# Causal mask of two attention stages: added by VectorE with the row maximum, in place of mask products on TensorE

## The chip, the cores and the metric

The kernel runs on one core of a Trainium2 chip. Five engines work side by side, each through its own queue in order: TensorE (PE in the profile; its weight loads are listed as PEld), VectorE (DVE), ScalarE (ACT), GpSimd (POOL), and SyncE (SP), which here only issues DMAs. They wait for each other by semaphores. The metric is the time of one execution on the device in microseconds (us); the kernel before has a median of 3226.27 us.

## The reference

Two transformer layers follow each other on x of 16 sequences x 512 tokens x 128 channels: a gated state-space block, a latent attention (16 heads of 8), a routed SwiGLU expert layer, a plain causal attention (16 heads of 8), a routed GELU expert layer, each with a residual and a layer norm. The two attentions are what the change touches:

```python
# latent attention (layer 0), kk and qq are [no-rope 4 | rope 4] per head
scores = jnp.einsum('bqhd,bkhd->bhqk', qq, kk) * scale
causal = jnp.tril(jnp.ones((S, S), dtype=bool))
scores = jnp.where(causal[None, None], scores, jnp.finfo(scores.dtype).min)
probs = jax.nn.softmax(scores, axis=-1)
y = jnp.einsum('bhqk,bkhd->bqhd', probs, v).reshape(B, S, H)
...
# plain attention (layer 1)
scores = jnp.einsum('bhqd,bhkd->bhqk', q, k)
causal = jnp.tril(jnp.ones((S, S), dtype=bool))
scores = jnp.where(causal[None, None], scores, jnp.asarray(MASK_BIAS, scores.dtype))
attn = jax.nn.softmax(scores.astype(jnp.float32), axis=-1).astype(dt)
ctx = jnp.einsum('bhqk,bhkd->bqhd', attn, v)
```

## The kernel before

The stages run one after the other. Both attentions are the function attention_stage: tiles named mla_... belong to the latent one, mha_... to the plain one. A sequence of 512 tokens is four blocks of 128 rows. The 16 heads are four groups g of four heads (NG = HG = 4), and one turn (one sequence) is the four groups in order; 16 turns make a stage, so a stage has 64 groups, two stages 128.

The softmax is done in two passes over the scores, one group apart and two groups apart:

- First pass, for group g: the products Q K^T with the queries as rows, cut to the causal width: row block j has w = 128 (j + 1) keys. They are 16 products (scores, L1394), packed into 11 units (UNITS1): unit 0 has four heads of 128 keys, units 1 and 2 two heads of 256, units 3 to 6 one head of 384, units 7 to 10 one head of 512. A unit fills one PSUM bank; three banks rotate (S1), so TensorE can be three units ahead of VectorE (semaphores s1_ready and s1_free). The last matmul of each unit (L1398) adds the causal mask: identity times a 128 x 128 triangle of 0 and -1e30, on the last 128 keys of every head of the unit. VectorE then takes the negated row maximum of every head in the bank by one TENSOR_REDUCE per unit (L1101) into nm.
- The maxima of the group are split by GpSimd into two parts (nhl), transposed by TensorE (L1441) to rows, copied by VectorE (mhl, L1068) and carried by a DMA into two further rows of Qb.
- Second pass, two groups later: K Q^T with the keys as rows and these two rows included, so that the score less its maximum comes out (scores_less_max, L1406), 16 products in 10 units (UNITS2), in two PSUM banks (s2_free, s2_ready). ScalarE takes the exponential (L1297), and GpSimd zeroes what lies above the diagonal (mask_unit, L1216); it is told by e_seen that an exponential is finished. Then come the products with V (times_v, L1414), a selection product that turns them back (L1446), and VectorE's division (normalise, L1073 and L1074).

The order on each engine is written out by hand. TensorE goes through k = 0 to 10 in each group and issues scores(k) and then scores_less_max(k). At k = 4 (WIDE) come the transposed maxima, the selection product and the first half of the products with V; at k = 8 the second half. The work that prepares the next sequence lies in between: in group 0 at k = 6 the latent projection (latent stage only), in group 1 at k = 0 and k = 6 the key and query projections and at k = 4 the output product, in group 2 at k = 7 the value projection, in group 3 at k = 4 a transpose of x. VectorE goes through the same k: the maximum of unit k, at k = 4 L1068, L1073 and L1074, and in between the rotation (turn_rows: L1052, L1053, L1055), the low parts (L1046, L1059, L1040), the output sum (L1086) and the statistics (L105, L108, L1035, L1036).

## Time and profile before

| | |
|---|---|
| median of 3 runs | 3226.27 us |
| lowest, highest | 3219.61, 3237.03 us |
| the profiled execution | 3232.98 us, its span 3231.2 us |
| TensorE, busy share of the span | 81% |
| VectorE | 67% |
| ScalarE | 44% |
| GpSimd | 36% |
| mean granted TensorE clock | 0.919 |

The span is the time from the first to the last instruction. "Busy" is the time in which at least one instruction's record is open on an engine; records of neighbouring instructions overlap, so the distance from one start to the next is shorter than a record. The latent attention lies between about 550 and 1385 us of the span, the plain one between about 1900 and 2690 us.

### The profile page before, as it was taken

How to read it: one execution, taken by the hardware profiler on the slowest of the kernel's cores; microseconds unless marked ns; L12 is line 12 of the kernel's file. 1: busy time of each engine (PE TensorE's matmuls, PEld its weight loads, DVE VectorE, ACT ScalarE, POOL GpSimd, SP SyncE). 2: the span in 40 equal slices, each digit the busy share in tenths (PEclk: the TensorE clock that was granted, in tenths of full speed). 3: DMA queues.
4: the chain of work that ended last, by engine and by line, in shares of the span. 5: the costliest groups of instructions: out<-in, count | busy, mean ns of one | idle time of the engine just before them, and what ended most of it. 6: DMA issues, size and time to landing. Idle time of an engine off the chain costs nothing. (4 is left out here: it accounts for less than half of the span.)

```text
span 3231.2 us, 51537 instructions
## 1 busy us (share of the span) xinstructions
PE 2618.4 (81%) x17479; PEld 2011.4 (62%) x17479; DVE 2178.6 (67%) x5628; ACT 1414.6 (44%) x2412; POOL 1177.9 (36%) x2298
## 2 busy tenths in 40 slices
PE   1445873999999999948888759999999997698972
PEld 1423662777777777636666647777777766486861
DVE  5733773777777767448888846676767754677785
ACT  0001330455555555511111225666666652586861
POOL 3210110334434344322222113454455442773076
PEclk9997995899999999969999969999999995799996
DMA  2144001213223222031110032222122114697772
GB/s 29 32 134 127 23 13 30 41 29 44 42 29 47 37 34 41 15 104 50 49 49 32 3 43 33 31 40 36 25 40 40 26 17 165 231 296 225 250 218 73
DMA packets 198657, 228.02 MB, mean 71 GB/s; under 512 B 48621, under 2 KB 148814, under 8 KB 190478
## 3 DMA queue, kind: packets, MB, share of 16 engines
q1 hardware_dynamic: 188302, 207.69, 26.7%
q0 software_dynamic: 8192, 16.79, 1.6%
q10 hardware_dynamic: 2048, 2.10, 0.2%
q8 instruction: 60, 0.98, 0.1%
q14 instruction: 55, 0.45, 0.0%
HBM read 132.55 MB, written 58.10 MB: 59 GB/s over the span
## 5 line engine op out<-in xcount | busy, mean ns | idle before, releaser
L1394 PE MATMUL banks<-Kb,Qb 96*128 96x128 f32 (+3 forms) x2048 | 599.6, 348 | 58.6 <-issue 27.3
L1406 PE MATMUL banks<-Qb,Kb 98*128 98x512 f32 (+3 forms) x2048 | 602.7, 356 | 4.8 <-ACT mha_prob L1297 1.0
L1101 DVE TENSOR_REDUCE mha_nm<-banks 128x1 f32<-128x384 f32 (+3 forms) x704 | 421.5, 639 | 185.9 <-PE banks L1398 172.3
L1101 DVE TENSOR_REDUCE mla_nm<-banks 128x1 f32<-128x384 f32 (+3 forms) x704 | 419.9, 638 | 160.0 <-PE banks L1398 146.5
L1297 ACT ACTIVATE mla_prob<-banks 128x512 f32<-128x512 f32 x640 | 376.5, 598 | 311.6 <-PE banks L1406 303.2
L1394 PEld LDWEIGHTS banks<-Kb,Qb 96*128 96x128 f32 x2048 | 364.3, 195 | 216.5 <-issue 159.9
L1297 ACT ACTIVATE mha_prob<-banks 128x512 f32<-128x512 f32 x640 | 375.7, 598 | 273.7 <-PE banks L1406 260.8
L1216 POOL TENSOR_SCALAR_AFFINE_SELECT mla_prob<-mla_prob 128x256 f32<-128x256 f32 (+1 forms) x640 | 237.8, 379 | 405.3 <-PE banks L1394 379.7
L1406 PEld LDWEIGHTS banks<-Qb,Kb 98*128 98x128 f32 x2048 | 334.8, 193 | 47.1 <-issue 7.6
L1216 POOL TENSOR_SCALAR_AFFINE_SELECT mha_prob<-mha_prob 128x256 f32<-128x256 f32 (+1 forms) x640 | 225.6, 361 | 355.4 <-PE banks L1394 329.2
L1828 PE MATMUL banks<-glu_wd,glu_hid 128*128 128x128 f32 x1024 | 147.7, 288 | 74.3 <-DVE glu_hid L1707 74.1
L1828 PEld LDWEIGHTS banks<-glu_wd,glu_hid 128*128 128x128 f32 x1024 | 130.5, 196 | 117.6 <-DVE glu_hid L1707 113.8
L2174 DVE TENSOR_TENSOR moe_hl<-moe_h,moe_hh 128x512 fp32r<-128x512 f32 x212 | 146.4, 692 | 78.7 <-ACT moe_h L2278 65.7
L1788 ACT ACTIVATE glu_sg<-banks 128x512 f32<-128x512 f32 x128 | 76.4, 597 | 262.2 <-PE banks L1802 262.2
L2277 ACT ACTIVATE moe_hh<-banks,moe_bt 128x512 fp32r<-128x512 f32 x212 | 146.1, 689 | 87.7 <-PE banks L2291 72.3
L1398 PE MATMUL banks<-mla_mask,mla_identr 128*128 128x128 f32 (+2 forms) x704 | 183.8, 261 | 0.0
L2227 POOL DMA_INDIRECT moe_gb<-results,moe_back_slot x128 | 131.2, 1025 | 143.5 <-SPq L1988 105.6
L1398 PE MATMUL banks<-mha_mask,mha_identr 128*128 128x128 f32 (+2 forms) x704 | 181.5, 258 | 0.0
L1414 PE MATMUL banks<-mla_prob,mla_V 128*9 128x512 f32 (+3 forms) x2048 | 169.1, 450 | 0.3
L1414 PE MATMUL banks<-mha_prob,mha_V 128*9 128x512 f32 (+3 forms) x2048 | 167.4, 446 | 0.2
L2214 POOL DMA_INDIRECT slots<-X,moe_slot x128 | 126.5, 988 | 67.3 <-issue 38.7
L1398 PEld LDWEIGHTS banks<-mla_mask,mla_identr 128*128 128x128 f32 x704 | 139.2, 198 | 8.5
(434 smaller groups left out, 5392.1 us busy)
## 6 DMA issues: line engine op xcount, KB each, us to landing
moe_wt<-expert_rows SPq DMA_DIRECT2D x53, 1024.0 KB
conv_tz<-conv_kernel SPq DMA_DIRECT2D x16, 1024.0 KB, 6.8
moe_xg<-slots SPq DMA_DIRECT2D x53, 256.0 KB
results<-moe_yt SPq DMA_DIRECT2D x53, 256.0 KB
Kb<-mla_kh SPq DMA_DIRECT2D x32, 256.0 KB, 4.9
Qb<-mla_qh SPq DMA_DIRECT2D x128, 64.0 KB
Kb<-mha_kh SPq DMA_DIRECT2D x32, 256.0 KB, 5.6
Qb<-mha_qh SPq DMA_DIRECT2D x128, 64.0 KB
```

The lines of the kernel that those rows point to most:

```text
L1101: dve.tensor_reduce(nm[:, g % 2, h:h + heads, j], ps[:, bank1(g, k), 0:heads * w].rearrange("p (h k) -> p h k", h=heads), axis=AX.X, op=AL ...
L1216: pool.affine_select(out=part, in_=part, compare_op=ALU.is_ge, fill=0.0, base=0, pattern=pattern, channel_multiplier=-1).then_inc(p_ready, 1)
L1297: act.activation(prob[:, g % 2, k, :], ps[:, S2 + k % 2, :], ACT.Exp, scale=HD ** -0.5).then_inc(s2_free, 1)
L1394: one = pe.matmul(ps[:, bank, x * w:(x + 1) * w], Qb[0:MROW, u, g, h + x, j * P:(j + 1) * P], Kb[0:MROW, u, g, 0:w], start=(x == 0), stop= ...
L1398: pe.matmul(ps[:, bank, 0:heads * w].rearrange("p (x w) -> p x w", x=heads)[:, :, w - P:w], identr[:, :], mask[:, 0:heads, :], start=False ...
L1406: last = pe.matmul(ps[:, S2 + k % 2, at:at + w], Kb[0:MROW + 2, u, grp, kb * P:(kb + 1) * P], Qb[0:MROW + 2, u, grp, h, kb * P:L], start=T ...
L1414: last = pe.matmul(ps[32 * hh:32 * hh + HD + 1, OB, kb * P:L], V[:, u, kb, grp * HG + hh, :], prob[:, par, unit, at:at + w], start=(kb == ...
L1828: last = pe.matmul(ps[:, OB + e % 2, b * P:(b + 1) * P], hid[:, e % 2, b * P:(b + 1) * P], wd[:, e, :], start=True, stop=True)
L2174: dve.tensor_tensor(hl[:, k, :], h[:, k, :], f32(hh[:, k, :]), ALU.subtract).then_inc(hid_ready, 1)
L2214: pool.indirect_dma_start(slots_d, bass.IndirectOffsetOnAxis(slot[:, q, a, t:t + 1], 0), X[:, first + j, b, :], None).then_inc(scattered[q ...
L2227: pool.indirect_dma_start(gb[:, j % 2, a, b, :], None, res_d[q], bass.IndirectOffsetOnAxis(back_slot[:, q, a, t:t + 1], 0)).then_inc(gathe ...
L2277: act.activation(hh[:, k, :], ps[:, FB + k, :], ACT.Gelu_apprx_tanh, bias=bias)
```

## The change

In scores the mask product and its constant tiles go: the identity identr and the four-fold mask. The products of a unit are now each a closed group of their own (start and stop both true), and the last one tells s1_ready. The mask becomes one tile of 128 x 512: zeros, and the triangle in the last 128 columns, so that its last w columns are the mask of any row block.

On VectorE the one TENSOR_REDUCE of a unit is replaced by one tensor_tensor_reduce for each head: it adds the last w columns of the mask to the head's scores from PSUM, multiplies by -1, and takes the minimum of that along the row, which is the negated maximum. The sum itself is written to a tile that nobody reads (junk, bfloat16). A unit's bank is freed with its last head. Such an instruction is compiled to two: the pass over the row, and one that writes the result to nm.

The signal e_seen, which rode on the first score product of the next unit, is now an instruction of its own on TensorE's queue, behind the wait for s2_free.

```diff
-        mask, identr = N.sb("mask", [P, HG, P], F32R), N.sb("identr", [P, P], F32R)
+        mask, junk = N.sb("mask", [P, L]), N.sb("junk", [P, 3, L], BF16)
...
-                sp.dma_start(maskf, io["c_mask"]).then_inc(consts, 16)
+                sp.dma_start(mask[:, L - P:L], io["c_mask"]).then_inc(consts, 16)
...
+                link(dve.memset(mask[:, 0:L - P], 0.0))
...
-                link(dve.tensor_copy(mask[:, :, :], maskf.unsqueeze(1).broadcast_to([P, HG, P])))
-                link(dve.tensor_copy(identr[:, :], ident[:, :]))
...
-                                w = P * (j + 1)
-                                dve.tensor_reduce(nm[:, g % 2, h:h + heads, j],
-                                                  ps[:, bank1(g, k), 0:heads * w].rearrange("p (h k) -> p h k", h=heads),
-                                                  axis=AX.X, op=ALU.max, negate=True).then_inc(s1_free, 1)
+                                w, bank = P * (j + 1), bank1(g, k)
+                                for x in range(heads):
+                                    last = dve.tensor_tensor_reduce(
+                                        junk[:, S1.index(bank), x * w:(x + 1) * w], ps[:, bank, x * w:(x + 1) * w],
+                                        mask[:, L - w:L], -1.0, BIG, ALU.add, ALU.min, nm[:, g % 2, h + x, j:j + 1])
+                                last.then_inc(s1_free, 1)
...
                     for x in range(heads):
                         one = pe.matmul(ps[:, bank, x * w:(x + 1) * w], Qb[0:MROW, u, g, h + x, j * P:(j + 1) * P],
-                                        Kb[0:MROW, u, g, 0:w], start=(x == 0), stop=False, skip_group_check=True)
-                        if seen and x == 0:
-                            one.then_inc(e_seen, 1)
-                    pe.matmul(ps[:, bank, 0:heads * w].rearrange("p (x w) -> p x w", x=heads)[:, :, w - P:w],
-                              identr[:, :], mask[:, 0:heads, :], start=False, stop=True,
-                              skip_group_check=True).then_inc(s1_ready, 1)
+                                        Kb[0:MROW, u, g, 0:w], start=True, stop=True)
+                    one.then_inc(s1_ready, 1)
...
                     pe.wait_ge(s2_free, c.next(s2_free))
+                    pe.sem_inc(e_seen, 1)
```

TensorE, latent stage, the last unit of group 0 and the first two of group 1 in one turn of the loop. Before:

```order
L1394 MATMUL banks<-Kb,Qb 128x512 [waits mla_s1_free]
L1398 MATMUL banks<-mla_mask,mla_identr 128x128
L1394 MATMUL banks<-Kb,Qb 128x128 [waits mla_s1_free,mla_m_rows1]
L1394 MATMUL banks<-Kb,Qb 128x128 x3
L1398 MATMUL banks<-mla_mask,mla_identr 128x512
L1406 MATMUL banks<-Qb,Kb 128x512 [waits mla_s2_free]
```

The same place of the changed kernel:

```order
L1396 MATMUL banks<-Kb,Qb 128x512 [waits mla_s1_free]
L1396 MATMUL banks<-Kb,Qb 128x128 [waits mla_s1_free,mla_m_rows1]
L1396 MATMUL banks<-Kb,Qb 128x128 x3
L1405 MATMUL banks<-Qb,Kb 128x512 [waits mla_s2_free]
```

The mask products between the first-pass products and the second-pass ones are gone; nothing else moved.

VectorE, latent stage, units 0 to 4 of group 1. Before:

```order
L1101 TENSOR_REDUCE mla_nm<-banks 128x4 [waits mla_s1_ready]
L1101 TENSOR_REDUCE mla_nm<-banks 128x2 [waits mla_s1_ready] x2
L1052 TENSOR_TENSOR mla_xs<-banks,mla_sinr 128x512 [waits mla_k_ready]
L1053 TENSOR_TENSOR mla_tmp<-banks,mla_cosr 128x512
L1055 TENSOR_TENSOR mla_tmp<-mla_tmp,mla_xs 128x512 [waits mla_done]
L1101 TENSOR_REDUCE mla_nm<-banks 128x1 [waits mla_s1_ready] x2
```

The changed kernel, from the second head of unit 2 on (the first head of a unit is the row with the wait; ISA is the name of the new instruction's two parts):

```order
L1102 ISA mla_junk,mla_nm<-banks,mla_mask 128x256 [waits mla_s1_ready]
L1102 ISA mla_nm 128x1
L1102 ISA mla_junk,mla_nm<-banks,mla_mask 128x256
L1102 ISA mla_nm 128x1
L1052 TENSOR_TENSOR mla_xs<-banks,mla_sinr 128x512 [waits mla_k_ready]
L1053 TENSOR_TENSOR mla_tmp<-banks,mla_cosr 128x512
L1055 TENSOR_TENSOR mla_tmp<-mla_tmp,mla_xs 128x512 [waits mla_done]
L1102 ISA mla_junk,mla_nm<-banks,mla_mask 128x384 [waits mla_s1_ready]
L1102 ISA mla_nm 128x1
L1102 ISA mla_junk,mla_nm<-banks,mla_mask 128x384 [waits mla_s1_ready]
L1102 ISA mla_nm 128x1
```

Where one row stood for a unit, two now stand for each of its heads: 32 instructions in a group for 11, at the same places between the other work.

## Rows read from the trace of the kernel before

**Rows 1.** The page: busy time of each engine, and its second part, 40 slices.
```profile
PE 2618.4 (81%) x17479; PEld 2011.4 (62%) x17479; DVE 2178.6 (67%) x5628; ACT 1414.6 (44%) x2412; POOL 1177.9 (36%) x2298
PE   1445873999999999948888759999999997698972
```

**Rows 2.** Windows, latent stage: groups 0 to 3 of one turn (columns: stretch, length, busy).
```profile
core 0: us, PE busy (x) PEld busy (x) DVE busy (x) ACT busy (x) POOL busy (x), PEclk, DMA share, GB/s
800.17:813.00 12.83, 12.83 (x98) 9.73 (x97) 8.63 (x17) 8.26 (x15) 3.75 (x12) 1.00 0.00 1
813.00:827.73 14.73, 13.92 (x105) 10.43 (x104) 12.34 (x23) 7.51 (x14) 5.01 (x14) 1.00 0.16 39
827.73:838.15 10.42, 10.42 (x86) 7.84 (x85) 9.41 (x26) 5.83 (x11) 7.39 (x16) 1.00 0.60 80
838.15:850.66 12.51, 11.72 (x95) 8.85 (x94) 7.97 (x15) 7.70 (x14) 5.45 (x18) 1.00 0.32 38
```

**Rows 3.** Windows, plain stage: groups 0 to 3 of one turn, same columns.
```profile
2131.02:2141.93 10.91, 10.91 (x90) 8.29 (x89) 7.33 (x14) 6.98 (x12) 3.75 (x12) 1.00 0.01 2
2141.93:2155.68 13.75, 13.49 (x105) 10.51 (x103) 10.63 (x26) 9.11 (x16) 4.03 (x13) 1.00 0.06 16
2155.68:2166.97 11.29, 11.29 (x93) 8.66 (x93) 7.30 (x14) 5.97 (x12) 9.96 (x22) 1.00 0.70 91
2166.97:2179.09 12.12, 11.33 (x92) 8.47 (x91) 7.98 (x16) 7.32 (x14) 5.03 (x16) 1.00 0.16 30
```

**Rows 4.** Timeline of TensorE: start, length, line; units with one head, latent stage.
```profile
844.96 0.40 PE L1394 MATMUL banks<-Kb,Qb 96*128 96x512 f32 x1
845.19 0.22 PE L1398 MATMUL banks<-mla_mask,mla_identr 128*128 128x128 f32 x1
845.25 0.48 PE L1406 MATMUL banks<-Qb,Kb 98*128 98x512 f32 x1
845.57 0.39 PE L1394 MATMUL banks<-Kb,Qb 96*128 96x512 f32 x1
```

**Rows 5.** The same view: a bare wait, then units with four and two heads.
```profile
837.04 0.22 PE L1398 MATMUL banks<-mla_mask,mla_identr 128*128 128x128 f32 x1
837.10 0.61 PE L1394 MATMUL banks<-Kb,Qb 96*128 96x128 f32 x4
837.55 0.45 PE L1398 MATMUL banks<-mla_mask,mla_identr 128*128 128x512 f32 x1
837.84 0.40 PE L1406 MATMUL banks<-Qb,Kb 98*128 98x512 f32 x1
...
838.32 0.28 PE L1398 MATMUL banks<-mla_mask,mla_identr 128*128 128x256 f32 x1
838.43 0.45 PE L1406 MATMUL banks<-Qb,Kb 98*128 98x128 f32 x2
```

**Rows 6.** Timeline of VectorE: runs of one instruction close behind each other.
```profile
833.07 0.38 DVE L108 BATCH_NORM_AGGREGATE mla_mv<-mla_st 128x2 f32<-128x6 f32 x4
833.48 0.32 DVE L1035 TENSOR_TENSOR mla_var<-mla_mv 128x4 f32<-128x4 f32 x1
833.84 0.16 DVE L1036 TENSOR_TENSOR mla_var<-mla_var,mla_mv 128x4 f32<-128x4 f32 x1
...
836.72 4.31 DVE L1101 TENSOR_REDUCE mla_nm<-banks 128x1 f32<-128x512 f32 x7 [0.59 <-PE banks L1398]
```

**Rows 7.** Groups of instructions, shapes apart: mean ns behind the comma, latent stage.
```profile
L1101 DVE TENSOR_REDUCE mla_nm<-banks 128x1 f32<-128x512 f32 x224 | 144.3, 684 | 47.4 <-PE banks L1398 44.1
L1101 DVE TENSOR_REDUCE mla_nm<-banks 128x1 f32<-128x384 f32 x223 | 117.3, 553 | 46.3 <-PE banks L1398 46.3
```

**Rows 8.** Timeline of VectorE in group 1, latent stage: where it waits.
```profile
814.59 1.34 DVE L1101 TENSOR_REDUCE mla_nm<-banks 128x2 f32<-128x512 f32 x2 [0.89 <-PE banks L1398]
...
820.74 1.08 DVE L1101 TENSOR_REDUCE mla_nm<-banks 128x1 f32<-128x384 f32 x2 [0.54 <-PE banks L1398]
822.17 0.69 DVE L1059 TENSOR_TENSOR mla_kl<-mla_tmp,mla_kh 128x512 fp32r<-128x512 f32 x1 [0.35 <-ACT mla_kh L1271]
```

**Rows 9.** The page's fifth part: first-pass products, and the time that TensorE waits.
```profile
L1394 PE MATMUL banks<-Kb,Qb 96*128 96x128 f32 (+3 forms) x2048 | 599.6, 348 | 58.6 <-issue 27.3
L1398 PE MATMUL banks<-mla_mask,mla_identr 128*128 128x128 f32 (+2 forms) x704 | 183.8, 261 | 0.0
L1101 DVE TENSOR_REDUCE mla_nm<-banks 128x1 f32<-128x384 f32 (+3 forms) x704 | 419.9, 638 | 160.0 <-PE banks L1398 146.5
```

11 lines of the change are left out of this document (5 added, 6 removed).

## The prediction

> **What bounds the kernel now.** First I read the busy shares and slices [rows 1]: TensorE leads with 81%, and its slices stand at 9 where the two attentions run. That share is no proof, since records of matmuls overlap, so the second view is the windows of one turn of each stage, group by group [rows 2, 3]. They show three kinds of group. In most of them TensorE is busy from edge to edge and VectorE has 3 to 4.5 us of air: latent groups 0 and 3 (12.83 and 12.51 us, VectorE busy 8.63 and 7.97), plain groups 0, 2 and 3 (10.91, 11.29, 12.12 us; 7.33, 7.30, 7.98). TensorE sets their length. In latent group 2 VectorE is busy 9.41 of 10.42 us: both are close. In latent group 1 VectorE is busy 12.34 of 14.73 us, and most of what is left is three waits of 0.89, 0.54 and 0.35 us [rows 8]; here VectorE's extra work (two rotations, low parts, output sum) sets the length. Plain group 1 lies between (10.63 of 13.75). So the change moves work from the engine that bounds five groups in eight to the one that bounds one or two.
>
> **What is removed on TensorE.** The record of a mask product is 0.26 us on average [rows 9], but that is no price: the next matmul starts inside it. From start to start a one-head mask product takes 0.06 us (845.19 to 845.25 [rows 4]), a two-head one 0.11 to 0.12, the four-head one 0.29 (837.55 to 837.84) [rows 5]. Per group: 8 x 0.06 + 2 x 0.12 + 0.29 = 1.0 us. That is the lower bound of the saving where TensorE is the bound. More may go: a second-pass product of 512 columns takes 0.32 us to the next start, a first-pass one of the same width 0.23 [rows 4]; the difference of 0.09 may be a weight load that the short mask product was too short to hide. If all of it went in 10 units the saving would be 1.9 us. I take 1.2, near the lower end, since only the directly read spacing is sure.
>
> **What is added on VectorE.** A run of seven maxima over 512 columns lasts 4.31 us [rows 6], and one record is 0.684 [rows 7], so they follow each other every (4.31 - 0.68) / 6 = 0.605 us. 128 columns more or less are 0.684 - 0.553 = 0.131 us [rows 7], or 1.02 ns a column, so the fixed part is 0.605 - 0.524 = 0.08 us. Columns per group stay the same, 5120. Instructions that pass over a row go from 11 to 16: 5 x 0.08 = 0.40 us. The trace has no instruction that adds and reduces at once; I price its pass like a plain one of the same columns, as both read one PSUM stream, with a second stream from SBUF beside it. New too are 16 writes of the result. The nearest row is a small instruction in a run: four of L108 last 0.38 us with about 0.15 each, so one every 0.08 us [rows 6]. The other bound is a write that overlaps with nothing: the pass is waited for to its record's end (0.684 in place of 0.605) and the write takes a whole small record, 0.16 as L1036 [rows 6], together 0.24. I take 0.08, because no write here has to wait for a semaphore and every run of unlinked instructions in the trace overlaps. 16 x 0.08 = 1.3 us. The addition is 1.7 us per group, 218 us of VectorE in 128 groups, against some 154 us taken off TensorE.
>
> The Trainium skill (VectorE: DVE Perf Modes, "Two Vector instructions with no wait between them") says that an instruction with an accumulator output is two instructions, and that each is held back only where an operand's start quadrant differs from the one used last; all operands here start at partition 0, so by that rule the write overlaps, as I take it. No row of before has such a pair.
>
> One more rule speaks against the change. The seven-fold run gives a fixed part of 0.08 us for a PSUM source [rows 6, 7]. The skill (Perfetto Trace Analysis, "Optimizing Scalar/DVE Operations") puts the overhead of a VectorE instruction at about 125 ns on PSUM. By that the five added passes would cost 0.63 us in place of 0.40; in the three groups where VectorE counts that is 0.7 us a turn, and the forecast would be 3160. The trace disagrees, and I stay with it.
>
> **The signal and the rest.** Ten times per group TensorE's queue now holds a bare wait for s2_free with the signal to GpSimd. A bare wait stands there already ahead of unit 0, and the product behind it starts 0.06 us after the one ahead (837.04 to 837.10 [rows 5]): nothing, as long as the exponential of two units before is done. Units last 0.5 to 0.7 us and an exponential is released two units back, so it is hidden; uncovered it costs at most the 0.05 us or so of a start, 0.5 us per group. GpSimd gets its signal earlier; it has 5 to 9 us of air per group [rows 2]. The constants at the stages' start are under 1 us.
>
> **Group by group.** VectorE's floor is its busy time + 1.7; TensorE's is the length - 1.2 where it sets it. Latent: group 0 12.83 -> 11.6 (VectorE's floor 10.3); group 3 12.51 -> 11.3 (9.7). Group 1: VectorE 12.34 + 1.7 = 14.0, and of its waits the first shrinks, since unit 0 now keeps VectorE 0.6 us longer while TensorE is in the key projection, and the second vanishes as the maxima of units 0 to 4 end later; about 1.0 us remains: 15.0, or +0.3. Group 2: 9.41 + 1.7 = 11.1, with 0.4 of air 11.5, or +1.1. Turn: -1.2 + 0.3 + 1.1 - 1.2 = -1.0 us. Plain: groups 0, 2 and 3 lose 1.2 each (VectorE's floors 9.0, 9.0, 9.7 against 9.7, 10.1, 10.9). Group 1: TensorE's floor 13.49 - 1.2 = 12.3, VectorE's 10.63 + 1.7 = 12.3; two equal loads leave air, I say 13.1, or -0.65. Turn: -4.3 us. With 15 full turns in each stage (the first and last are partial) the sum is 15 x 5.3 = 80 us. The profiled execution took 3232.98 us, so 3153; it was 7 us above the median of 3226.27, so the forecast for a median is 3146 to 3153. I write 3150.
>
> **Rivals.**
> 1. Slower: the write isn't overlapped. At 0.24 us in place of 0.08 for each of 16 pairs VectorE gets 2.5 us more per group, 4.2 in all. Floors: latent 12.8, 16.5, 13.6, 12.2, sum 55.1; with 1 us of air the turn is 5.6 above 50.5. Plain: 11.5, 14.8, 11.5, 12.2, sum 50.0, with 1.5 of air 3.4 above 48.1. 15 x 9 = +135 us: 3360. It turns from gain to loss where a write costs about 0.14 us (5.3 / 14.3 of the way). For it: nothing in the trace has such a pair. Against it: every unlinked run overlaps.
> 2. No change: three banks aren't enough to keep TensorE free. VectorE now needs 0.69 us for a unit of one head and 512 columns, TensorE about 0.5 to 0.55, so TensorE is stopped at every fourth unit, and in turn VectorE stands still during products with V. TensorE waits for VectorE already, a part of the 58.6 us [rows 9]. If two thirds of the gain in the TensorE groups is lost this way (0.4 left of 1.2), the turns change by +0.6 and -1.6 us, 15 us in all; with a few tenths for the bare waits it is zero: 3225.
> 3. Larger: the hidden weight loads go too (1.9 for 1.2). The five TensorE groups give 0.5 more each where VectorE's floor allows it, 15 x 2.3 = 35 us: 3115.
>
> **How the numbers follow.** Forecast 0.54 (own range 3130 to 3195), rival 3 0.08, rival 2 0.18 (3195 to 3245), rival 1 0.20, a third of it between 3240 and 3260 for a write of 0.14 to 0.17 us. The range 3095 to 3260 leaves out most of rival 1 (0.13) and the far end of rival 3 (0.03). Runs tell about 0.5% from no change, 16 us: faster holds the forecast, rival 3 and a quarter of rival 2, 0.67; same 0.12; slower 0.21.
>
> **What the changed profile would show.** VectorE's run of one-head units of 512 columns spaced 0.68 to 0.70 us (rival 1: 0.82 or more); the small write of nm 0.08 us before the next start. TensorE from a first-pass product of 512 columns to the second-pass one 0.23 us. Group lengths as above: latent group 1 and 2 not shorter, plain groups 0 and 2 shorter by a microsecond. The wait of L1396 for VectorE several times what it was; if it eats more than 0.5 us of each TensorE group, rival 2 is it. The prediction is wrong if a pass with two sources costs more per column than 1.02 ns, or if the granted clock, 1.00 in all eight windows [rows 2, 3], drops because TensorE has more air.

## The result, and the profile after

The changed kernel takes 3301.05 us (median of 4 runs, 3282.12 to 3304.74) against 3226.39 us: 1.0217 times as long, with a 95% interval of 1.0168 to 1.0265. A repetition in other runs gave 1.0195 (1.0122 to 1.0269). It is slower; 3150 us and a gain of 2.4% had been forecast. The page of the changed kernel, busy times, slices and three groups:

```profile
PE 2622.3 (79%) x16071; PEld 1894.3 (57%) x16071; DVE 2228.2 (67%) x8314; ACT 1389.0 (42%) x2412; POOL 1157.3 (35%) x2298
...
PEclk9997995898878989969999959899888996799996
...
L1396 PE MATMUL banks<-Kb,Qb 96*128 96x128 f32 (+3 forms) x2048 | 623.6, 364 | 96.9 <-DVE mla_nm L1102 44.2
L1405 PE MATMUL banks<-Qb,Kb 98*128 98x512 f32 (+3 forms) x2048 | 600.9, 357 | 34.4 <-ACT mla_prob L1299 11.5
...
L1102 DVE CUSTOM_DVE_ANT_0 mla_junk<-banks,mla_mask 128x128 bf16<-128x128 f32 (+3 forms) x1024 | 446.2, 487 | 187.3 <-PE banks L1396 156.5
```

TensorE has 1408 matmuls fewer (two stages of 64 groups with 11 mask products), and yet its busy time is 2622.3 us where it was 2618.4 [rows 1]. The products L1396 are 623.6 us in place of 599.6 and their waits 96.9 in place of 58.6 [rows 9]; those of the second pass wait 34.4 us (L1405) in place of 4.8 (L1406 before). Between the eighth and the fifteenth and between the twenty-sixth and the thirty-first slice, where the attentions run, the granted clock reads 8 in nine places and 7 in one; the same line of the kernel before has nines in these places but for the 8 of the eighth:

```profile
PEclk9997995899999999969999969999999995799996
```

The next view says how much that is. Windows over the latent and the plain stage, first of the kernel before, then of the changed one (both from repeated runs on one chip; columns: stretch, length, busy times, clock, DMA):

```profile
553.40:1341.40 788.00, 765.05 (x5722) 576.20 (x5721) 598.83 (x1205) 444.13 (x785) 320.25 (x842) 0.97 0.24 36
1892.70:2639.80 747.10, 733.73 (x5708) 561.94 (x5706) 521.24 (x1057) 450.73 (x785) 340.64 (x898) 0.99 0.22 33
```

```profile
552.10:1386.40 834.30, 767.72 (x5019) 516.32 (x5018) 626.50 (x2549) 433.35 (x785) 308.03 (x842) 0.89 0.23 35
1938.60:2703.40 764.80, 724.30 (x5004) 490.98 (x5003) 544.27 (x2401) 437.43 (x785) 334.24 (x898) 0.92 0.23 33
```

The two stages are 64.0 us longer, about what the whole is (spans of 3222.6 and 3283.8 us; 58.5 us between the medians of all runs of both kernels on that occasion). The mean granted clock fell from 0.97 and 0.99 to 0.89 and 0.92. The clock has two levels, 1.2 and 2.4 GHz, so TensorE ran at the lower one for 41 and 22 us before, and for 180 and 121 us after. One turn of the changed kernel shows where, in windows of its four groups (plain stage, same columns):

```profile
2387.57:2397.93 10.36, 10.27 (x78) 6.78 (x79) 7.11 (x34) 6.27 (x12) 3.84 (x12) 1.00 0.01 2
2397.93:2409.97 12.04, 11.66 (x89) 8.40 (x87) 10.49 (x48) 8.22 (x15) 3.83 (x12) 1.00 0.00 1
2409.97:2424.89 14.92, 14.14 (x85) 9.62 (x86) 7.97 (x37) 6.17 (x12) 10.06 (x22) 0.77 0.58 83
2424.89:2438.68 13.79, 11.91 (x78) 6.92 (x77) 9.39 (x40) 8.16 (x15) 4.67 (x14) 0.88 0.21 27
```

Group 2 of this turn had 6.8 us at half clock and lasts 14.92 us; group 2 at full clock lasts 11.96. So a microsecond at half clock costs 3.0 / 6.8 = 0.44 us. The same sum over all groups with a fall, in all traces of this study, has the median 0.44, with half of the groups between 0.41 and 0.55; for the changed kernel the median is 0.42. I take 0.43. What got longer can be read off the products with V, 3.12 us in place of 1.69, on TensorE, first in group 2 above, then in a group at full clock:

```profile
2416.52 3.12 PE L1413 MATMUL banks<-mha_prob,mha_V 128*9 128x512 f32 x16
...
2217.26 1.69 PE L1413 MATMUL banks<-mha_prob,mha_V 128*9 128x512 f32 x16
```

Now the loss has two parts that must be looked at apart, and every run below is read in the same way. **Turn at full clock**: the length of each kind of group, from TensorE's first product of unit 0 to that of the next group, as the median over those groups in which the clock didn't fall; four of them make a turn. **Half clock**: the time at 1.2 GHz within a stage. For the changed kernel against the one before (12.24, 13.91, 11.76, 11.44 and 10.82, 13.12, 11.91, 11.43 us before):

| group | latent: forecast | measured | plain: forecast | measured |
|---|---|---|---|---|
| 0 | -1.2 | -0.83 | -1.2 | -0.48 |
| 1 | +0.3 | -0.44 | -0.65 | -1.09 |
| 2 | +1.1 | +0.24 | -1.2 | +0.05 |
| 3 | -1.2 | +0.11 | -1.2 | -0.04 |
| turn | -1.0 | -0.92 | -4.3 | -1.56 |

Latent group 2 of the changed kernel was at full clock only three times, so its +0.24 rests on these. At full clock the change gains 2.5 us in two turns, 16 x 2.5 = 40 us, half of the forecast 80. The clock takes (180 + 121 - 41 - 22) x 0.43 = 102 us. The sum is +62, measured +64.

### The profile page after: what moved, and what is told of

It reads as the page before. It is cut to its first block and busy times, and to the rows that moved or that the text cites. A ratio compares the mean times of both kernels' runs of the same rounds, so it can differ in the third digit from the quotient of the medians.

```text
span 3303.0 us, 52641 instructions
## 1 busy us (share of the span) xinstructions
PE 2622.3 (79%) x16071; PEld 1894.3 (57%) x16071; DVE 2228.2 (67%) x8314; ACT 1389.0 (42%) x2412; POOL 1157.3 (35%) x2298
## 5 line engine op out<-in xcount | busy, mean ns | idle before, releaser
L1396 PE MATMUL banks<-Kb,Qb 96*128 96x128 f32 (+3 forms) x2048 | 623.6, 364 | 96.9 <-DVE mla_nm L1102 44.2
L1405 PE MATMUL banks<-Qb,Kb 98*128 98x512 f32 (+3 forms) x2048 | 600.9, 357 | 34.4 <-ACT mla_prob L1299 11.5
L1102 DVE CUSTOM_DVE_ANT_0 mha_junk<-banks,mha_mask 128x128 bf16<-128x128 f32 (+3 forms) x1024 | 443.5, 487 | 196.0 <-PE banks L1396 180.9
L1102 DVE CUSTOM_DVE_ANT_0 mla_junk<-banks,mla_mask 128x128 bf16<-128x128 f32 (+3 forms) x1024 | 446.2, 487 | 187.3 <-PE banks L1396 156.5
L1396 PEld LDWEIGHTS banks<-Kb,Qb 96*128 96x128 f32 x2048 | 378.1, 203 | 294.6 <-issue 170.7
L1405 PEld LDWEIGHTS banks<-Qb,Kb 98*128 98x128 f32 x2048 | 389.1, 205 | 147.3 <-issue 124.6
L1413 PE MATMUL banks<-mla_prob,mla_V 128*9 128x512 f32 (+3 forms) x2048 | 192.7, 500 | 0.0
L1413 PE MATMUL banks<-mha_prob,mha_V 128*9 128x512 f32 (+3 forms) x2048 | 188.0, 490 | 0.0
L2275 ACT ACTIVATE moe_h<-banks,moe_bt 128x512 f32<-128x512 f32 x212 | 144.3, 681 | 0.0
L1685 DVE SCALAR_TENSOR_TENSOR glu_acc<-banks,glu_wts,glu_acc 128x128 f32<-128x128 f32 x448 | 125.4, 342 | 0.2 <-PE banks L1825 0.2
L2286 PE MATMUL banks<-moe_xth,moe_wt 128*128 128x512 f32 x212 | 95.0, 448 | 35.1 <-DVE moe_xtl L2026 35.1
```

The costliest lines, as they stand in the source:

```text
L1102: last = dve.tensor_tensor_reduce(junk[:, S1.index(bank), x * w:(x + 1) * w], ps[:, bank, x * w:(x + 1) * w], mask[:, L - w:L], -1.0, BIG, ...
L1396: one = pe.matmul(ps[:, bank, x * w:(x + 1) * w], Qb[0:MROW, u, g, h + x, j * P:(j + 1) * P], Kb[0:MROW, u, g, 0:w], start=True, stop=True)
L1405: last = pe.matmul(ps[:, S2 + k % 2, at:at + w], Kb[0:MROW + 2, u, grp, kb * P:(kb + 1) * P], Qb[0:MROW + 2, u, grp, h, kb * P:L], start=T ...
L1413: last = pe.matmul(ps[32 * hh:32 * hh + HD + 1, OB, kb * P:L], V[:, u, kb, grp * HG + hh, :], prob[:, par, unit, at:at + w], start=(kb == ...
L2275: act.activation(h[:, k, :], ps[:, FB + k, :], ACT.Gelu_apprx_tanh, bias=bias).then_inc(h_ready, 1)
```

## The experiments

In the first four texts the names of theories are those that each explains; from the fifth on A is ScalarE and the two banks of the second pass, B is VectorE and its three banks, C the clock, and D and S are explained where they stand. All runs, with the ratio to the kernel before on the same occasion. Stages, half clock and turns are read from one traced execution; the last column is from all executions: the half clock of the whole program, 2 x (1 - mean granted clock) x span, its median less that of the kernel before, in us.

| run | ratio, 95% interval | stages, us | half clock, us | turn at full clock, us | half clock, all |
|---|---|---|---|---|---|
| before (b_again) | 1.0019 (1.0000, 1.0038) | 788.0 / 747.1 | 41 / 22 | 49.3 / 47.3 | +7 |
| changed (a_again) | 1.0195 (1.0122, 1.0269) | 834.3 / 764.8 | 180 / 121 | 48.4 / 45.7 | +226 |
| e1_masks_kept | 1.0171 (1.0126, 1.0216) | 835.1 / 769.1 | 87 / 43 | 50.3 / 48.2 | +68 |
| e2_no_mask_products | 0.9997 (0.9972, 1.0023) | 804.1 / 735.4 | 160 / 71 | 47.7 / 45.5 | +172 |
| e3_hybrid | 1.0030 (1.0004, 1.0055) | 819.3 / 736.6 | 160 / 36 | 48.7 / 46.3 | +125 |
| e4_filler | 1.0240 (1.0186, 1.0294) | 872.1 / 760.1 | 237 / 67 | 49.0 / 47.1 | +232 |
| b_exp_half | 0.9932 (0.9910, 0.9954) | 776.4 / 734.8 | 33 / 12 | 48.8 / 46.8 | -16 |
| a_exp_half | 1.0052 (1.0026, 1.0077) | 831.7 / 734.9 | 210 / 100 | - / 44.2 | +231 |
| h1_groups_0_1 | 1.0184 (1.0161, 1.0206) | 854.0 / 745.3 | 194 / 60 | 48.8 / 46.2 | +192 |
| h2_group_1 | 1.0043 (1.0020, 1.0066) | 791.7 / 744.3 | 50 / 38 | 49.4 / 46.8 | +65 |
| h3_masks_0_2 | 1.0224 (1.0194, 1.0255) | 871.8 / 749.3 | 226 / 46 | 49.4 / 47.0 | +199 |
| h4_masks_1_3 | 1.0249 (1.0225, 1.0274) | 859.8 / 762.1 | 205 / 64 | - / 47.1 | +199 |
| i1_new_signal | 1.0005 (0.9992, 1.0018) | 787.6 / 748.9 | 30 / 12 | 49.7 / 47.7 | -10 |
| i2_old_signal | 1.0204 (1.0181, 1.0227) | 832.9 / 760.6 | 190 / 128 | 48.2 / 45.3 | +266 |
| i3_group_1 | 1.0032 (1.0011, 1.0054) | 821.6 / 736.5 | 129 / 34 | 49.3 / 46.4 | +72 |
| j1_plain_1 | 0.9952 (0.9937, 0.9967) | 782.6 / 738.6 | 30 / 40 | 49.4 / 46.4 | -3 |
| j2_plain_1_03 | 0.9946 (0.9929, 0.9962) | 782.7 / 726.3 | 30 / 34 | 49.4 / 45.8 | +13 |

A dash: latent group 2 was at full clock only in the last turn, where part of its work is missing. On the occasions of the e, h and j runs the kernel before takes 3370 us in place of 3226. The excess lies behind the attentions: in j1 the plain stage starts at 1892.9 us (1892.7 in b_again), and from its end to the end of the span it is 723 us (583). What brings it stays open: the h runs (3370) and the i runs (3226) carry the same chip number. The places of the units in a group agree to 0.01 or 0.02 us between occasions where the code is the same, so lengths of groups and stages are compared freely, ratios only within one occasion. Half clock differs between executions of one kernel: 301 us in the trace a_again, 355 in the first trace of the changed kernel. A difference of 50 us between two traces is therefore no finding by itself, and three traces are of the fastest of twelve executions (h2, i1, j2).

### Mask products and VectorE, each alone

e1_masks_kept: the changed kernel with the mask products back (the mask is added twice).

```diff
                     for x in range(heads):
                         one = pe.matmul(ps[:, bank, x * w:(x + 1) * w], Qb[0:MROW, u, g, h + x, j * P:(j + 1) * P],
-                                        Kb[0:MROW, u, g, 0:w], start=True, stop=True)
-                    one.then_inc(s1_ready, 1)
+                                        Kb[0:MROW, u, g, 0:w], start=(x == 0), stop=False, skip_group_check=True)
+                    pe.matmul(ps[:, bank, 0:heads * w].rearrange("p (x w) -> p x w", x=heads)[:, :, w - P:w],
+                              identr[:, :], maskr[:, 0:heads, :], start=False, stop=True,
+                              skip_group_check=True).then_inc(s1_ready, 1)
```

> The changed kernel with its VectorE part as it is, but with the mask products put back on TensorE, so that TensorE does the work of before and VectorE that of after (the mask is added twice, which leaves the maxima as they are). Theory C (the loss of the change is TensorE's clock): the time at half clock in the two attentions, 355 us in after and 68 in before, goes back to under 120, and the kernel gets faster than after although it does more: 3225 to 3260 us. Theory V (the loss is that VectorE's units got longer and three banks do not cover it): work is added to TensorE and none taken off VectorE, so 3300 us or more.

e2_no_mask_products: the kernel before without them and with the new signal, VectorE as before. The maximum here is of the unmasked scores.

```diff
-                    pe.matmul(ps[:, bank, 0:heads * w].rearrange("p (x w) -> p x w", x=heads)[:, :, w - P:w],
-                              identr[:, :], mask[:, 0:heads, :], start=False, stop=True,
-                              skip_group_check=True).then_inc(s1_ready, 1)
+                    one.then_inc(s1_ready, 1)
```

> TensorE as in after, VectorE as before: the mask products are left out and the maximum is taken by the one reduction per unit over all columns, the causal mask left out of it (the maxima are then those of unmasked rows; the rest of the attention is the same); the signal to GpSimd as in after. Theory C: TensorE's columns are those of after, so the half clock comes as in after, over 200 us in the attentions, and the time is 3250 to 3300. Theory V: VectorE is that of before, so what I forecast for TensorE shows in full: 3130 to 3170.

Both hold the new signal to GpSimd, so with i1 below (the kernel before with that alone) and the changed kernel they make a square. Half clock in both stages: 42 us with neither part (i1), 130 with VectorE's (e1), 231 with TensorE's (e2), 301 with both. Two turns at full clock: 97.3, 98.5, 93.2, 94.1 us. So taking the mask products away brings 170 to 190 us of half clock and gains 4.1 to 4.4 us of two turns; VectorE's part brings 70 to 90 us and costs 0.9 to 1.2. The last column of the table agrees: -10, +68, +172, +226. e1, with all columns kept, is 1.7% slower by VectorE's part and the signal, and e2 pays its gain of 3.4 us in two turns, 55 us in all, back to the clock (0.9997). So neither text was right in its times: by theory C e1 should have been faster than the changed kernel (1.0171 against 1.0195 can't be told apart) and e2 slower than the kernel before, by theory V e2 should have gained all that was forecast. The important number is that of e2: with VectorE wholly as before, and TensorE rid of 11 instructions in each group, the groups are the same as in the changed kernel where the forecast expected its largest gain: plain group 0 lasts 10.36 us against 10.34, and unit by unit TensorE stands at the same hundredths. What holds TensorE there isn't VectorE.

### Where VectorE does count

e3_hybrid: units 0 to 2 as before (mask products and one TENSOR_REDUCE), units 3 to 10 as changed.

```diff
+                                if k < TTR:
+                                    last = dve.tensor_reduce(nm[:, g % 2, h:h + heads, j],
...
+                                for x in range(heads if k >= TTR else 0):
                                     last = dve.tensor_tensor_reduce(
```

> Units 0 to 2 (several heads) as before, with mask product and one reduction; units 3 to 10 (one head each) as in after. VectorE issues no pass more than before; TensorE drops 8 mask products of 128 columns per group. Theory C: half of the mask columns are gone, half-clock time in the attentions between 100 and 300 us, time 3230 to 3290. Theory V: no unit on VectorE is longer, so TensorE's 8 x 0.06 us are gained in its groups: 3180 to 3215.

Its time and its half clock (1.0030, 196 us) are what theory C gave it.

In plain group 2 the changed kernel waits at units 2 and 3. TensorE, then VectorE, in a group at full clock:

```profile
2213.92 0.50 PE L1396 MATMUL banks<-Kb,Qb 96*128 96x256 f32 x2 [0.34 <-DVE mha_nm L1102]
2214.26 0.39 PE L1405 MATMUL banks<-Qb,Kb 98*128 98x512 f32 x1
2215.03 0.44 PE L1396 MATMUL banks<-Kb,Qb 96*128 96x384 f32 x1 [0.38 <-DVE mha_nm L1102]
```

```profile
2214.47 0.29 DVE L1102 CUSTOM_DVE_ANT_0 mha_junk<-banks,mha_mask 128x128 bf16<-128x128 f32 x1
2214.68 0.08 DVE L1102 DVE_READ_ACCUMULATOR2_ANT mha_nm<- 128x1 f32 x1
2214.68 0.29 DVE L1102 CUSTOM_DVE_ANT_0 mha_junk<-banks,mha_mask 128x128 bf16<-128x128 f32 x1
2214.89 0.09 DVE L1102 DVE_READ_ACCUMULATOR2_ANT mha_nm<- 128x1 f32 x1
2214.89 0.42 DVE L1102 CUSTOM_DVE_ANT_0 mha_junk<-banks,mha_mask 128x256 bf16<-128x256 f32 x1
...
2224.52 0.08 DVE L1102 DVE_READ_ACCUMULATOR2_ANT mha_nm<- 128x1 f32 x1
2224.52 0.69 DVE L1102 CUSTOM_DVE_ANT_0 mha_junk<-banks,mha_mask 128x512 bf16<-128x512 f32 x1
2225.13 0.08 DVE L1102 DVE_READ_ACCUMULATOR2_ANT mha_nm<- 128x1 f32 x1
```

Passes of 128 columns follow every 0.21 us, so the bank of unit 0 (four heads) is held for 3 x 0.21 + 0.29 = 0.92 us from the first start, where one instruction with a record of 0.68 us stood before. Unit 3 needs that bank: it starts at 2215.03, just behind the last pass (2214.68 + 0.29). The wait at unit 2 is for the last unit of the group before: VectorE had the low parts ahead of it (L1059, from 2212.08) and began its maximum at 2213.16. From unit 2 to unit 3 TensorE now takes 1.11 us, before 0.76. With units 0 to 2 as before (e3) plain group 2 is 11.58 us in place of 11.96, latent group 2 11.51 in place of 12.00, and groups 0 and 1 are longer (10.59, 12.48) by the mask products. Rival 2 of the forecast, that three banks are not enough, is thus real, in group 2.

### ScalarE sets the pace of the early units

The four runs b_again, a_again, b_exp_half and a_exp_half were made for this. The edit in the last two, made alike in the kernel before and in the changed one, leaves the second half of each block of probabilities stale:

```diff
-                                act.activation(prob[:, g % 2, k, :], ps[:, S2 + k % 2, :], ACT.Exp,
+                                cut = L if turn == "first" else L // 2
+                                act.activation(prob[:, g % 2, k, 0:cut], ps[:, S2 + k % 2, 0:cut], ACT.Exp,
```

> The kernel before, unchanged, for a trace from the same chip as the three that follow. Group lengths at full clock (from TensorE's first product of unit 0 to the next group's) should be those already read: latent 12.24, 13.92, 11.76, 11.44 us, plain 10.82, 13.13, 11.90, 11.44. Theory C (the clock): at most 100 us of the two attentions at half clock (68 in the first trace). If instead it shows 250 us or more here, the half clock of the changed kernels belongs to the chip and not to the change.

> The changed kernel, unchanged, same chip. Theory C: 300 to 400 us of the two attentions at half clock, at about 0.43 us lost for each of them, so 100 to 140 us lost against the kernel before, less about 40 us won at full clock: slower by 60 to 100 us, 1.02 to 1.03 times. Rival: VectorE's longer first units alone cost the time; then the groups at full clock, not the half-clock ones, must be longer than those of the kernel before.

> The kernel before; from the second sequence on ScalarE's exponential covers 256 of 512 columns, so that the other half of the probabilities is stale. All else, and every matmul, is as it was. Theory A (with the mask products there TensorE itself sets the pace of a unit, 0.58 to 0.69 us against ScalarE's 0.60): groups 0 and 3 move by 0 to 0.3 us, the turns by under 1 us, 10 to 30 us in all. Rival B (VectorE sets it): no change at all.

> The changed kernel with the same half-width exponential. Theory A (without the mask products the two banks of the second pass and ScalarE's 0.60 us set the pace; it is why only 0.45 of 1.35 us per group came): at full clock plain group 0 falls from 10.35 to about 9.5 us, latent group 0 from 11.42 to about 10.9, group 3 by 0.5 or more, and the sums of a turn by 1.5 to 3 us. Rival B (VectorE and its three banks set it): groups 0 and 3 stay within 0.15 us of 10.35, 11.42, 11.4 and 11.8. On the clock: if TensorE's waits bring the half clock, it stands at half clock for less than the changed kernel does on the same chip, by a third or more; if the fewer columns bring it, for as long or longer.

Both unchanged kernels came as expected, the changed one at the lower edge (58.5 us slower, 301 us at half clock). With the short exponential, plain group 0 of the kernel before goes from 10.82 to 10.70 us, of the changed one from 10.34 to 9.73; latent group 0 from 12.24 to 12.22 and from 11.41 to 11.03; group 3 of the changed kernel from 11.55 and 11.39 to 10.95 and 10.97. The gain from the change is then 12.22 - 11.03 = 1.19 us in latent group 0 (1.08 if only every second turn is compared, since the changed kernel was at full clock in those alone) and 0.97 in plain group 0, near the forecast's 1.2. Theory A holds and B falls for group 0; plain group 2 moves by 0.25 only, there it is VectorE. In group 3 the short exponential takes 0.28 us off the kernel before too (11.44 and 11.43 to 11.15), so the change still gains no more than 0.20 and 0.18 there: exponentials are not all that holds it.

The rows that say it stand in the trace of the kernel before. ScalarE at the start of plain group 3 (from 2204.77), kernel before (b_again):

```profile
2204.67 0.60 ACT L1297 ACTIVATE mha_prob<-banks 128x512 f32<-128x512 f32 x1 [0.95 <-PE banks L1406]
2205.16 0.59 ACT L1301 ACTIVATE mha_osb<-banks 128x512 f32<-128x512 f32 x1
2205.64 0.60 ACT L1288 ACTIVATE mha_V<-banks 128x512 f32<-128x512 f32 x1
2206.12 1.80 ACT L1297 ACTIVATE mha_prob<-banks 128x512 f32<-128x512 f32 x3
```

The changed kernel at the same place (a_again, group 3 from 2360.06), ScalarE and then TensorE:

```profile
2360.02 0.60 ACT L1299 ACTIVATE mha_prob<-banks 128x512 f32<-128x512 f32 x1 [0.84 <-PE banks L1405]
2360.51 0.59 ACT L1303 ACTIVATE mha_osb<-banks 128x512 f32<-128x512 f32 x1
2360.99 0.60 ACT L1290 ACTIVATE mha_V<-banks 128x512 f32<-128x512 f32 x1
2361.47 1.10 ACT L1299 ACTIVATE mha_prob<-banks 128x512 f32<-128x512 f32 x2
```

```profile
2361.27 0.40 PE L1396 MATMUL banks<-Kb,Qb 96*128 96x256 f32 x2
2362.23 0.47 PE L1405 MATMUL banks<-Qb,Kb 98*128 98x512 f32 x1 [0.56 <-ACT mha_prob L1299]
2362.54 0.34 PE L1396 MATMUL banks<-Kb,Qb 96*128 96x384 f32 x1
```

ScalarE works without a gap from 2204.67 on: two copies and then exponentials, 0.5 to 0.6 us apart. TensorE needed 0.58 to 0.65 us for a unit of one or two heads with its mask product, so the two kept step, and neither waited visibly. Without mask products TensorE is at unit 2 after 1.21 us where it took 1.62, and then stands before the second-pass product until 2362.23: unit 3 starts 2.48 us into the group, later than the 2.36 of before. ScalarE's share of 44% [rows 1] says nothing of this; its air lies in other parts of the group. With the short exponential unit 3 starts 2.21 us into the group before the change and 2.20 behind it, just behind the two copies in both.

The other thing that holds group 3 is its end. The first product of the next turn waits for VectorE's maximum of unit 9, the last unit but one (`back` in scores). TensorE, kernel before (its first trace, that of the rows), the first product behind a plain group 3:

```profile
2177.82 0.63 PE L1394 MATMUL banks<-Kb,Qb 96*128 96x128 f32 x4 [0.79 <-DVE mha_nm L1101]
```

This wait is 0.30 and 0.80 us alternately, from one sequence to the next, and 0.41 and 1.20 us in the changed kernel: the last unit starts 0.06 us earlier there (10.58 us into the group for 10.64), and the wait for VectorE gives it back.

### The place of the mask columns, and filler

e4_filler: the changed kernel, second-pass products of units 1 to 3 issued twice.

```diff
-                    for h, kb, at, w in UNITS2[k]:
+                    for h, kb, at, w in UNITS2[k] * (2 if k in (1, 2, 3) else 1):
```

> The changed kernel, with the second-pass products of units 1 to 3 issued twice on TensorE (the second overwrites the first with the same), 1536 columns more in each group, at a place where TensorE of after waits for VectorE. Theory C: half-clock time in the attentions falls to under 150 us and the kernel gets faster than after: 3200 to 3260. Theory V: nothing is won, at most the wait is filled: 3300 to 3340.

h3_masks_0_2 and h4_masks_1_3: the changed kernel with the mask products of e1 in groups 0 and 2, or in 1 and 3, alone. h1_groups_0_1 and h2_group_1: the whole change made in groups 0 and 1, or in group 1, alone (TENSOR_REDUCE and mask product elsewhere, new signal everywhere).

```diff
+                    if g in MASKS:
+                        one = pe.matmul(ps[:, bank, 0:heads * w].rearrange("p (x w) -> p x w", x=heads)[:, :, w - P:w],
+                                        identr[:, :], maskr[:, 0:heads, :], start=False, stop=True,
+                                        skip_group_check=True)
                     one.then_inc(s1_ready, 1)
```

> The change made in groups 0 and 1 alone; groups 2 and 3 keep the mask products and one TENSOR_REDUCE per unit. At full clock latent groups 0 to 3 should last 11.41, 13.47, 11.76, 11.44 us, plain ones 10.34, 12.03, 11.90, 11.43: 1.27 and 1.57 us less per turn than before, 45 us in 32 turns. Theory C (mask columns taken away near where the clock falls bring the half clock): with two groups of four left as they were the half-clock time lies between that of before (63 us in the attentions) and that of the full change (301), about 180: a loss of 50 us, so 0.99 to 1.01. Rival D (the half clock comes from VectorE's longer first units in group 2, where TensorE waits for it): it stays under 100 us and the kernel is faster, 0.985 to 0.99.

> The change made in group 1 alone. Group 1 falls to 13.47 (latent) and 12.03 us (plain), the other three stay: 0.44 and 1.09 us less per turn, 24 us in all at full clock. Theory C: half clock in the attentions 60 to 140 us, most of it where group 2 begins in the latent one; 0.993 to 1.003. Rival D: 63 us as before, 0.993.

> The changed kernel with VectorE's new instruction everywhere, and the mask products back in groups 0 and 2 alone (there the mask is added twice, which changes nothing in the maximum). At full clock a latent turn should last 12.28 + 13.47 + 12.17 + 11.55 = 49.5 us, a plain one 46.7. If the place of the columns matters (the half clock began 1 to 5 us into groups 0 and 2, nearly never in 1 and 3), half clock in the attentions falls from 301 to 100 to 170 us. If only the number of columns matters, it is the same here as in the next kernel, about 200.

> The same with the mask products back in groups 1 and 3 alone: as many columns as in the kernel before this one, elsewhere. At full clock a latent turn should last 11.41 + 14.10 + 12.00 + 11.77 = 49.3 us, a plain one 47.2. If the place matters, half clock stays at 220 to 300 us and this kernel is slower than the one with them in groups 0 and 2; if only the number matters, both show about 200.

In the changed kernel most falls begin 1 to 5 us into group 0 or 2 and last 6.8 or 10.2 us. That columns at these places would steer the clock held only in part, and e4, h1 and h3 missed what that theory gave them, h2 by a little in its time. Putting columns back in groups 0 and 2 left the latent stage at 226 us, in 1 and 3 at 205, filler at 237: none better than the 180 and 206 of the two traces of the changed kernel. In the plain stage all of them helped (46, 64 and 67 us against 121 and 148); whether the place counts there can't be told from 46 and 64 in one trace each. With two groups changed (h1) the latent stage is as bad as with four, 194 us. With group 1 alone (h2) it is 50 in the trace, but that is the fastest of twelve executions; the median of h2 has 65 us more half clock in the whole program than the kernel before, h1 192, the changed kernel 226. So half clock isn't proportional to what is taken away: two groups of four cost nearly as much as all.

What TensorE did before a fall can be read from the traces. The 6 us ahead of a fall in latent group 2 of the changed kernel (a_again), then the same place in the kernel before (b_again; columns as above):

```profile
1152.70:1158.70 6.00, 4.45 (x32) 2.97 (x25) 5.68 (x24) 3.74 (x8) 2.32 (x8) 1.00 0.62 94
```

```profile
1070.33:1076.33 6.00, 5.19 (x38) 4.09 (x31) 5.72 (x9) 3.90 (x8) 3.37 (x8) 1.00 0.62 94
```

TensorE's records are open in 74% of this stretch, and in 86% before the change; the missing time is waits, up to 0.93 us, and most of them are for VectorE. In group 0 the falls come behind the wait at the end of group 3:

```profile
1181.29 0.63 PE L1396 MATMUL banks<-Kb,Qb 96*128 96x128 f32 x4 [1.20 <-DVE mla_nm L1102]
```

The clock fell at 1182.6. In both stages of a_again (all turns from the third on), a group 0 that opens with the longer of the two waits had a fall in 11 cases of 14, one with the shorter wait in none of 14. But such waits are no sufficient cause: j2 has waits of up to 1.2 us at this place and no fall behind them. And a_exp_half, in which the early units wait less, has 310 us of half clock against 301.

The Trainium skill (TensorE: Matmul & The Clock Gate, "Part 1: The HAM clock gate") says that the clock is set by how busy the array has been of late, the low level being the default, and has it fall after an idle stretch. The direction agrees: less issued, 301 us for 63, and waits ahead of the falls. But these are short (the longest ahead of each fall is 0.3 to 1.3 us in a_again), and between them TensorE works. What exactly must be missing for a fall isn't settled by these runs.

### The signal to GpSimd

i0_before is the kernel before again: 3226.66 us, stages 788.1 and 749.0 us.

> The kernel before, unchanged, for a trace from the same chip as the next three. Runs of it gave 3226 us with one pair of calls and 3370 with another. If it gives 3370 here, its attentions should still last about 790 and 746 us and the other 140 us should lie outside them; then the group lengths of all runs can be compared with each other, whatever the time of the whole. If the attentions are the longer part, they can't.

i1_new_signal: the kernel before with the new signal alone. i2_old_signal: the changed kernel, signal moved ahead of the wait for ScalarE. The edit of i2:

```diff
                     one.then_inc(s1_ready, 1)
+                    if seen:
+                        pe.sem_inc(e_seen, 1)
...
                     pe.wait_ge(s2_free, c.next(s2_free))
-                    pe.sem_inc(e_seen, 1)
```

> The kernel before with one part of the change alone: the signal to GpSimd is an instruction of its own between the wait for ScalarE and the second-pass product. Mask products and VectorE as before. Theory S (it lengthens the way from one exponential to the next, which sets the pace in places): groups 0, 2 and 3 become 12.28, 11.95, 11.72 us (latent) and 10.95, 12.07, 11.73 (plain), as in the kernel with group 1 alone changed; 0.5 and 0.6 us more per turn, about 18 us in all, 1.004 to 1.008. The forecast's term (nothing): 12.24, 11.76, 11.44 and 10.82, 11.90, 11.43; 1.000.

> The changed kernel with the signal ahead of that wait, behind the next unit's first-pass products. Theory S: the waits of TensorE at units 3, 5 and 8 shrink (plain group 0: unit 2 to 3 takes 0.72 us, 7 to 8 0.78 in the changed kernel), the group falls from 10.35 to 10.1 to 10.2 us, the turns by 0.3 to 0.8 us at full clock, 10 to 25 us in all, unless the clock takes it: 1.01 to 1.02 times before in place of 1.02. The forecast's term: no difference from the changed kernel.

TensorE between the first products of units 2 and 3 of plain group 0, first changed kernel, then i2:

```profile
2191.03 0.40 PE L1396 MATMUL banks<-Kb,Qb 96*128 96x256 f32 x2
2191.44 0.48 PE L1405 MATMUL banks<-Qb,Kb 98*128 98x512 f32 x1
2191.76 0.34 PE L1396 MATMUL banks<-Kb,Qb 96*128 96x384 f32 x1
```

```profile
2457.42 0.41 PE L1396 MATMUL banks<-Kb,Qb 96*128 96x256 f32 x2
2457.73 0.50 PE L1406 MATMUL banks<-Qb,Kb 98*128 98x512 f32 x1
2458.07 0.34 PE L1396 MATMUL banks<-Kb,Qb 96*128 96x384 f32 x1
```

0.73 us became 0.65. At each place where TensorE waits for an exponential, the signal between wait and product lengthens the way by 0.06 to 0.08 us; where it doesn't wait, nothing changes. Group 3 of the kernel before gets 0.29 us longer by it (11.44 to 11.73), plain group 0 0.14; two turns are 0.7 us longer (i1), and 0.7 us shorter in i2. The time of the whole did not follow: i1 is at 1.0005 (0.9992, 1.0018), where 1.004 to 1.008 was expected. Its traced stages had 22 us less of half clock than those of i0, worth 9 us against the 11 lost at full clock; but the median execution has only 10 us less, so part of the miss stays unexplained. i2 is no better than the changed kernel, since half clock stays at 318 us. So the term is real and too small to matter.

### A version that beats both

i3_group_1: the kernel before with the change in group 1 alone in both stages, and the signal of i2. j1_plain_1: the same in the plain stage alone. j2_plain_1_03: and units 5 to 10 of the plain groups 0 and 3. The edit of j2:

```diff
+        def by_dve(g, k):
+            return not latent and (g == 1 or (g in (0, 3) and k > 4))
...
+                                if not by_dve(g, k):
+                                    last = dve.tensor_reduce(nm[:, g % 2, h:h + heads, j],
...
+                                for x in range(heads if by_dve(g, k) else 0):
+                                    last = dve.tensor_tensor_reduce(
```

> The change in group 1 alone, where TensorE is given the most to do beside the scores, with the signal placed as in the run before this one. Groups 0, 2 and 3 as in the kernel before, group 1 at 13.4 (latent) and 12.0 us (plain): 0.5 and 1.1 us less per turn, 25 us. Half clock in the attentions 60 to 100 us (88 with group 1 alone and the signal as changed). 0.991 to 0.996, faster than both kernels. If the clock takes the gain, 0.997 to 1.003 and over 120 us of half clock.

> The change in group 1 of the plain stage alone, with the signal ahead of the wait; the latent stage keeps its mask products. In the kernel with group 1 changed in both stages the plain stage got 12.5 us shorter at 34 us of half clock (24 before), and the latent one 33.5 us longer at 129 us (41 before). If the two stages don't act on each other: 12 us less, 0.996, and half clock 75 us or less in both attentions. The other way: the clock falls in the latent stage here too, and the time is 1.00.

> The same, and in groups 0 and 3 of the plain stage units 5 to 10 (one head each) are changed as well; units 0 to 4, behind which the clock has fallen, keep their mask products. At full clock plain group 0 falls from 10.84 to about 10.5 us, group 3 from 11.44 to 11.2, beside 1.1 of group 1 and 0.1 given back in group 2: 1.5 us per turn, 22 us in all, 0.993, if half clock in the plain stage stays under 40 us. If it rises as the columns go (6 x 128 more gone in each of two groups), to 80 us or more, the gain is gone: 0.998 to 1.003.

i3 came by its second branch, in which the clock takes the gain: the plain stage won 12.5 us as thought, but the latent one had 129 us of half clock. h2, which differs by the place of the signal, had 50 in its trace; yet that trace is the fastest of its twelve executions and the one of i3 the second slowest, and the medians are alike (+65 and +72 us in the whole program, 1.0043 and 1.0032). Without the latent part both versions are faster than both kernels, by half a per cent: 0.9952 (0.9937, 0.9967) and 0.9946 (0.9929, 0.9962). Windows over the stages of j2 beside those at the head of this document:

```profile
554.70:1337.40 782.70, 759.27 (x5722) 572.56 (x5721) 595.72 (x1205) 444.52 (x785) 307.20 (x842) 0.98 0.24 37
1888.40:2614.70 726.30, 709.78 (x5339) 516.76 (x5338) 526.18 (x1585) 440.88 (x785) 339.21 (x898) 0.98 0.23 34
```

The plain stage is 20.8 us shorter than in the kernel before at nearly its clock, with 369 matmuls less. The latent stage, 5.3 us shorter, has the signal's place as its one difference, and 11 us less of half clock. The gain of the whole is 0.5%, and j2's lead on j1 is within the intervals.

## Why the prediction was wrong

**The clock: the step that failed.** The sum took durations at a granted clock of 1.00 and kept it there, since all eight windows showed 1.00 [rows 2, 3]. The text named the fall among the things that would make it wrong, but gave it neither price nor chance. It costs 102 us where the whole gain forecast was 80. The kernel before had already had falls in the two attentions, 41 and 22 us; windows over the whole stages would have shown them.

**What a mask product costs** (1.2 us per group, bounds 1.0 to 1.9): right in size. Where the next wait is taken away 1.0 to 1.2 us came out. From unit to unit the changed kernel is 0.23, 0.12 and 0.11 us quicker for four, two and one head, 1.35 us over a group if nothing else held it.

**Who sets the length of groups 0 and 3: wrong.** "TensorE is busy from edge to edge and VectorE has 3 to 4.5 us of air" compared two engines, and busy was read from records that overlap [rows 4], which hide waits of a tenth or two. For group 3 the rows themselves said otherwise: 11.72 of 12.51 us and 11.33 of 12.12 [rows 2, 3] leave 0.79 us idle, the wait for VectorE at the end of the group. The third engine, ScalarE, was dismissed with "an exponential is released two units back, so it is hidden". It was hidden only because the mask products filled the time: ScalarE's own rate, one every 0.6 us, stood directly behind. So 0.48 in place of 1.2 in plain group 0, and nothing in group 3, where two copies come first and the wait for VectorE last.

**What VectorE gets** (+1.7 us per group): four times too much. Passes of 512 columns still follow every 0.61 us (2224.52 and 2225.13 above) and the accumulator read starts together with the next pass: no time at all where 0.08 us each had been taken. Only the five added passes are left, 0.4 us; VectorE's busy time rose by 49.6 us in 128 groups, 0.39 each. The Trainium skill's rule (VectorE: DVE Perf Modes, "Two Vector instructions with no wait between them") agrees that the read isn't held back; it names no cost. This error made latent group 2 and both groups 1 come out worse in the forecast than they were: +0.24 for +1.1, -0.44 for +0.3, -1.09 for -0.65. Rival 1, with 0.24 us a write, falls. Rival 3, the weight loads, is seen in the 0.11 us of a one-head unit against 0.06 read, and changed nothing.

**Plain group 2** (-1.2, measured +0.05) is rival 2, with its mechanism and its place: the bank of the four-head unit is held 0.92 us.

**The signal** (nothing): 0.06 to 0.08 us at each place that waits for ScalarE, 0.7 us in two turns; below what the times can tell. A slip in rival 2 as well: three plain groups that lose 0.8 us each leave -1.9 us of the turn's -4.3, not -1.6, so its price was 20 us and not 15.

Two errors were of opposite sign and partly cancelled: the latent turn, -0.92 for -1.0, looks right and is right for wrong reasons.

## What to carry to other kernels

Before work is taken off the engine that seems to be the bound, look at the timeline of every other engine over the same units: one that runs in an unbroken chain, however low its share, is the next bound, and the saving stops there. On TensorE ask as well what the removal does to the granted clock: a stage that is full of small products and already shows a few falls may lose more by the clock than by the work, so change one group or stage at a time and read the mean clock of each stage with the time.

## What the runs showed of the hardware

- The result of a tensor_tensor_reduce is written by an instruction of 0.08 us that starts together with the next pass; passes with a PSUM and an SBUF source follow every 0.21, 0.34, 0.48 and 0.61 us for 128, 256, 384 and 512 columns, the same rate as a plain reduction of one source.
- The granted clock of TensorE halved, for mostly 6.8 or 10.2 us, behind stretches of 6 us in which TensorE's records were open 74 to 90% of the time (a_again, full turns; 4.45 of 6.00 us in the one shown) and no single wait was longer than 1.3 us. The same kernel had 301 us of them in one execution and 355 in another.
- A signal given between a wait and the product behind it adds 0.06 to 0.08 us to that way when the wait is a real one, nothing when it isn't.
- The same program took 3226 us on some occasions and 3370 on others; the difference lies whole in the part behind the plain attention (583 and 723 us), and its cause stays open.
